# Outer spectrum stored row by row, the inner transform and the mixing in 128-channel pieces, and a new order of steps

## The reference, cut to what matters

```
# layer 0, per image: 7x7 depthwise convolution, LayerNorm over channels, two linear maps with GELU, residual
h = conv7x7(x) + b;  h = LN(h);  x = (gelu(h @ w1 + b1) @ w2 + b2) * layer_scale + x
# layer 1, on tokens t (3136 x 96)
z = relu(bn1(LN(t) @ w1))                       # 3136 x 192
X = fft(z, axis=tokens, norm='ortho')
xr = relu(X.real * rd - X.imag * id + rb)       # rd, id: one number per channel (192)
xi = relu(X.imag * rd + X.real * id + ib)
y = ifft(xr + 1j * xi).real
t = t + bn2(y @ w2)                             # 192 -> 96 channels
t = t + qlinear(relu(qlinear(LN(t), W1)), W2)   # 96 -> 384 -> 96 with fp8 roundings
```

## Time and profile before

| what | value |
|---|---|
| median of 3 runs | 4494.48 us (4490.79 to 4496.14) |
| profiled execution, its own time | 4496.04 us |
| its span in the profile | 4494.2 us |
| PE, DVE, ACT, POOL busy | 4006.1, 3307.4, 2254.2, 1840.4 us |
| mean granted TensorE clock | 0.948 |

### The profile page before, as it was taken

The page is one execution under the profiler, slowest core; times in us unless marked ns, Lnnn a source line. Parts: engine busy times, 40 slices in busy tenths (PEclk is TensorE's granted clock), DMA queues, the critical chain, the costliest instruction groups (busy, mean ns, idle before and its releaser), DMA issues.

```text
span 4494.2 us, 88363 instructions
## 1 busy us (share of the span) xinstructions
PE 4006.1 (89%) x22802; PEld 2904.3 (65%) x22802; DVE 3307.4 (74%) x10713; ACT 2254.2 (50%) x4610; POOL 1840.4 (41%) x2468
## 2 busy tenths in 40 slices
PE   5999958899999999999999999999999999999986
PEld 3444435676666766676667676666666667676764
DVE  2333335688888888888888888888888888888877
ACT  2433423455555555555555555555555555555543
POOL 1111163444444444444444444444444444444431
PEclk9999979999999999999999999999999999999986
DMA  6566633444444444434444444444444444444331
GB/s 174 161 164 176 168 93 89 109 118 118 117 119 117 120 118 116 111 103 111 111 115 112 109 111 111 116 118 120 118 115 119 115 120 120 117 115 115 109 98 53
DMA packets 420415, 532.47 MB, mean 118 GB/s; under 512 B 220047, under 2 KB 378493, under 8 KB 404413
## 3 DMA queue, kind: packets, MB, share of 16 engines
q1 hardware_dynamic: 405920, 510.40, 42.4%
q10 hardware_dynamic: 14272, 20.04, 1.8%
HBM read 295.18 MB, written 235.12 MB: 118 GB/s over the span
## 4 chain that ended last, share of the span: by engine, by line
PE 29%; DVE 26%; DMA 13%; issue 10%; ACT 3%; SPq 2%; POOL 1%; DVEq 1%; ACTq 0%; POOLq 0%
DMA inner<-outer_spectrum 6%; PE psum L989 6%; DMA outer_spectrum<-outer 6%; DVE stats L823 5%; PE psum L1009 5%; PE psum L1028 4%; PE psum L995 4%; DVE minus L898 4%; DVE plus L898 3%; DVE t L859 3%; PE psum L1037 2%; DVE h L932 2%; DVE xn L925 2%; PE psum L1017 2%; DVE act L881 2%
## 5 line engine op out<-in xcount | busy, mean ns | idle before, releaser
L684 POOL TENSOR_TENSOR scales<-sums,minus_half 112x4 f32<-112x4 f32 (+1 forms) x480 | 605.8, 1266 | 1686.2 <-DVE sums L839 1685.7
L726 POOL TENSOR_TENSOR both<-plus,minus 96x224 f32<-96x224 f32 (+1 forms) x1024 | 642.7, 653 | 356.6 <-DVE minus L898 297.8
L781 ACT ACTIVATE uw<-psum,spec 96x224 f32<-96x224 f32 (+1 forms) x1024 | 449.4, 512 | 397.9 <-PE psum L1028 395.9
L989 PE MATMUL psum<-hn,w_sb 96*128 96x448 f32 x1344 | 566.3, 559 | 31.8 <-ACT hn L747 31.8
L995 PE MATMUL psum<-hid,w_sb 128*96 128x448 f32 x1344 | 554.7, 549 | 2.1 <-ACT hid L762 2.0
L762 ACT ACTIVATE hid<-psum,b_sb 128x448 f32<-128x448 f32 x672 | 421.3, 634 | 233.3 <-PE psum L989 192.0
L387 PE MATMUL c_psum<-c_xt,c_toeplitz 128*112 128x448 f32 x1152 | 477.9, 552 | 49.2 <-ACT c_xt L329 26.0
L1028 PE MATMUL psum<-inner_dft,inner 112*96 112x112 f32 x3712 | 431.2, 271 | 90.5 <-DMA inner<-outer_spectrum 89.8
L415 DVE TENSOR_SCALAR c_h<-c_psum,c_bias 112x448 f32<-112x448 f32 x192 | 199.0, 1037 | 415.1 <-PE c_psum L387 415.1
L701 POOL TENSOR_SCALAR h_norm<-h,sums,scales 112x96 f32<-112x96 f32 x896 | 461.3, 531 | 103.2 <-PE psum L982 102.9
L1028 PEld LDWEIGHTS psum<-inner_dft,inner 112*96 112x96 f32 x3712 | 406.0, 173 | 110.9 <-issue 86.4
(11 more groups left out here) (85 smaller groups left out, 6615.0 us busy)
## 6 DMA issues: line engine op xcount, KB each, us to landing
outer_spectrum<-outer SPq DMA_DIRECT2D x448, 168.0 KB
inner<-outer_spectrum SPq DMA_DIRECT2D x32, 2016.0 KB
c_xpad<-x SPq DMA_DIRECT2D x96, 392.0 KB, 11.2
h_tokens<-c_h SPq DMA_DIRECT2D x24, 1568.0 KB, 8.4
h<-h_tokens SPq DMA_DIRECT2D x32, 1176.0 KB, 13.9
x_sb<-x SPq DMA_DIRECT2D x32, 1176.0 KB, 7.7
residual_stream<-t SPq DMA_DIRECT2D x224, 168.0 KB, 2.0
inner_inverse<-unmixed SPq DMA_DIRECT2D x224, 168.0 KB, 2.3
```

Source lines behind the costliest of these rows:

```text
L684: nc.gpsimd.tensor_tensor(scales[which][:, at:at + w], su[:, :, 5], minus_half[:, 0:w], ALU.pow).then_inc(ready.sem, 1)
L726: last = nc.gpsimd.tensor_tensor(both[:, c % 2, m, 0:w, k * PT // 2:(k + 1) * PT // 2], half(plus), half(minus), ALU.subtract if k else AL ...
L781: last = nc.scalar.activation(uw[:, j % 2, k, 0:w * PT // 2].rearrange("p (s k) -> p s k", s=w), re, ACT.Identity, bias=spec[:, m, shift:s ...
L989: pe.matmul(bank("M1", c, m, CW, 128), w1_sb[:, m * 128:(m + 1) * 128], hn[:, c * CW:(c + 1) * CW], start=True, stop=True).then_inc(m1_mad ...
```

## The change

Six things are changed together.

1. `outer_spectrum` in DRAM becomes (28 q, 116 rows, 192) in place of (114 rows, 28 q, 192). The rows of the outer transform are laid out so that 29 rows that belong to one partition of `inner` follow each other. A store of a chunk of A is two transfers in place of three (pieces of 768 B in place of 3072 B). The load of `inner` is two transfers in place of three: 8 rows (6144 B for each of 112 partitions), then 21 rows (16128 B each), in place of 4 rows, 24 rows and one row in pieces of 768 B.
2. B works on two rows at a time, whose 2 x 192 channels are cut in three blocks of 128: channels 0 to 127 of the first row, the last 64 of the first with the first 64 of the second, the last 128 of the second (three "kinds"). There are 12 steps of up to four blocks of one kind: 44 matmuls for a turn in place of 58, and 12 steps on ACT, DVE and POOL in place of 16, on 128 partitions in place of 96.
3. W sums the kinds: for two rows a matmul of 96 columns from kind 0, one of 96 columns from kind 2 and one of 192 columns from kind 1 (its weights have zeros in half of the rows for each output). 44 matmuls in place of 58: 30 of 96 columns and 14 of 192.
4. The outer transform has 116 columns in place of 114.
5. The table of the outer transform is loaded in the convolution's first microseconds, between the loads of the first and the second part of x, and put in the new order by four DVE copies; the small weight loads are some more (55 in place of 42).
6. `STAGES` and `LATER` have new numbers throughout.

```diff
-    g_dram = nc.dram_tensor("outer_spectrum", (2 * K1, NQ, H2), F32, kind="Internal").ap()
+    g_dram = nc.dram_tensor("outer_spectrum", (NQ, ROWS, H2), F32, kind="Internal").ap()
...
-    2: {"B": (8.0, 8.7, ND), "W": (18.0, 9.9, ND), "IB": (27.5, 8.9, ND)},
+    2: {"B": (0.5, 4.7, KINDS * NG), "W": (18.0, 9.9, ND), "IB": (32.5, 8.7, ND)},
...
-    "sp": {"M2": -2.0, "IB": -0.5, "A": 12.0, "FETCH": -8.0, "FETCH NEXT": 10.5},
+    "sp": {"M2": 20.5, "IB": 2.5, "A": 7.0, "FETCH": -6.5, "FETCH NEXT": 12.5},
...
-                        for rows, part in ((slice(0, PT, 2), slice(0, K1 - 1)), (slice(1, PT, 2), slice(K1, 2 * K1 - 1)),
-                                           (slice(PT, 2 * K1), slice(K1 - 1, 2 * K1, K1))):
-                            sp.dma_start(g_dram[rows, CH * c:CH * c + CH, :], outer[part, c % 2, :, :]
+                        for rows in (slice(0, PT), slice(PT, ROWS)):
+                            sp.dma_start(g_dram[CH * c:CH * c + CH, rows, :].rearrange("q m h -> m q h"), outer[rows, c % 2, :, :]
                                          ).then_inc(outer_stored[c % 2].sem, 16)
...
-                        for part, (first, end) in enumerate(((0, CH), (CH, NS - 1))):
-                            rows = bass.AP(g_dram.tensor, first * PT * H2, [[H2, PT], [PT * H2, end - first], [1, H2]])
-                            sp.dma_start(inner[:, first:end, :], rows).then_inc(inner_loaded[part].sem, 16)
-                        sp.dma_start(inner[0:2 * NQ, NS - 1, :], g_dram[2 * K1 - 2:2 * K1, :, :].rearrange("m q h -> (m q) h")
-                                     ).then_inc(inner_loaded[1].sem, 16)
+                        spectrum = g_dram.rearrange("q (r s) h -> (q r) (s h)", s=NS)
+                        first = 2 * PAIRS * H2
+                        for part, columns in enumerate((slice(0, first), slice(first, NS * H2))):
+                            sp.dma_start(inner[:, columns], spectrum[:, columns]).then_inc(inner_loaded[part].sem, 16)
...
-                        w = chunk_pairs(c)
-                        for m in range(2):
-                            dst = bank("B", c, m, w * PT, C, "spec")
-                            for s in range(w):
-                                last = pe.matmul(dst[:, s * PT:(s + 1) * PT], inner[:, CH * c + s, m * C:(m + 1) * C],
-                                                 inner_dft[:, :], start=True, stop=True)
-                            last.then_inc(spec_made.sem, 1)
+                        w = blocks(g, kind)
+                        dst = bank("B", c, 0, w * PT, 128, "spec")
+                        for u in range(w):
+                            at = 128 * (KINDS * (PAIRS * g + u) + kind)
+                            last = pe.matmul(dst[:, u * PT:(u + 1) * PT], inner[:, at:at + 128], inner_dft[:, :],
+                                             start=True, stop=True)
+                        last.then_inc(spec_made.sem, 1)
...
+                        for u in range(chunk_pairs(c) // 2):
+                            two = dst[:, u * H2:(u + 1) * H2]
+                            pe.matmul(two[:, 0:C], both[:, g % 2, 0, first + u, :], aw2_sb[:, 0:C], start=(u == 0), stop=False)
+                            pe.matmul(two[:, C:H2], both[:, g % 2, 2, first + u, :], aw2_sb[:, C + H2:], start=False, stop=False)
+                            last = pe.matmul(two, both[:, g % 2, 1, first + u, :], aw2_sb[:, C:C + H2], start=False,
+                                             stop=(u == PAIRS // 2 - 1))
```

More of the change, by code:

```diff
@@ L25 @@
 ND = (NS + CH - 1) // CH
+NG = (ND + 1) // 2
+PAIRS = 4
+KINDS = 3
+ROWS = 4 * NS
 CC = 4
@@ L46, in chunk_pairs, with blocks @@
     return min(CH, NS - CH * d)
+def blocks(g, kind):
+    pairs = min(PAIRS, NS // 2 - PAIRS * g)
+    return pairs + (NS % 2 if g == NG - 1 and kind < 2 else 0)
 class Signal:
@@ L407, in _ @@
             dve.wait_ge(consts_loaded, 32)
+            dve.wait_ge(transform_loaded, 16)
+            columns = transform.rearrange("p (q m) -> p q m", m=2 * K1)
+            for j in range(2):
+                for part_ in range(2):
+                    at, count = NS * (2 * j + part_), NS - j
+                    nc.vector.tensor_copy(wts.outer_dft[0:PT, :, at:at + count],
+                                          columns[:, :, K1 * part_ + j:K1 * (part_ + 1):2])
+                    if j:
+                        nc.vector.memset(wts.outer_dft[0:PT, :, at + count:at + NS], 0.0)
             def part(n, g, slot, has_next, has_second):
@@ L489, in image_phase @@
         t1_fetched = [signal(f"t1_fetched{k}", len(range(k, NC, 3)), 16, first=2) for k in range(3)]
-        outer_stored = [signal(f"outer_stored{n}", 4 - n, 48) for n in range(2)]
-        inner_loaded = [signal(f"inner_loaded{part}", 1 + part, 16) for part in range(2)]
+        outer_stored = [signal(f"outer_stored{n}", 4 - n, 32) for n in range(2)]
+        inner_loaded = [signal(f"inner_loaded{part}", 1, 16) for part in range(2)]
         unmixed_stored = [signal(f"unmixed_stored{n}", ND // 2, 16, first=1) for n in range(2)]
@@ L1031, in turn @@
-                    if name == "W":
-                        w = chunk_pairs(c)
-                        dst = bank("W", c, 0, w * C, PT)
-                        pe.wait_ge(both_done.sem, both_done.at(n, 2 * c + 1))
-                        for s in range(w):
-                            for m in range(2):
-                                last = pe.matmul(dst[:, s * C:(s + 1) * C], both[:, c % 2, m, s, :],
-                                                 aw2_sb[:, m, :], start=(m == 0), stop=(m == 1))
+                        g, kind = c // KINDS, c % KINDS
@@ L1225, in fold_batch_norms @@
     count = 1
-    for bn, sc, half in ((raw.bn1, raw.scale1, raw.halves[:, :]), (raw.bn2, raw.scale2, raw.halves[0:C, 0:C])):
+    for bn, sc, half in ((raw.bn1, raw.scale1, raw.halves[0:PT, :]), (raw.bn2, raw.scale2, raw.halves[:, 0:C])):
         steps = [
```

181 lines of the change are left out of this document (97 added, 84 removed), and 6 rows, old and new, of the table LATER.

## The result

The changed kernel takes 4603.35 us, median of 4 runs (4600.73 to 4624.78), the kernel before 4495.31 in the same comparison (4490.79 to 4496.47). The ratio is 1.025, 95% interval 1.0225 to 1.0274: 2.5% slower. The forecast was 4542, with 4400 to 4605 as its range. The direction came out, and so did the mechanism at the turn's start; of the span's growth, 106.3 us (4600.5 for 4494.2), the forecast had 48.

A forecast was written before the change was run, and what follows sets the result against it. PE's work was taken to bound the long part, the order of transfers the turn's start. 4496 + 54 for 30 turns - 7 for other turns + 1 for the convolution's start gave 4544, as runs' median 4542; range 4400 to 4605.

The forecast's parts named there:

- What bounds the kernel: A turn has a long part, where PE's list sets the time, and a start, where the order of transfers counts.
- The line: Turn's start: x_sb, `back`, A6's store, `inner` and t_old land in series; S20 starts 31.2 us after A5's matmuls end.
- I take 11.0: Turn's start: the load of `inner` takes 11.0 us, with 9.5 as the range's lower value, where before it took 12.3.
- The long part: From S20 to the end of A5's matmuls: 87.3 us, with PE barely ahead of DVE.
- The turn: Turn's start 31.2 plus long part 87.3 gives 118.5 us for 116.7; 30 turns give +54.
- The ends: Turns without the long line save about 7 us in all; the convolution's start costs +1.
- A: Rival, turn's start: shorter transfers bring S20 at 27.5 us after A5's matmuls; 113.8 us a turn, 4403; chance 0.38.
- B: Rival, whole turn: both effects cancel, S20 at 29.6 us after A5's matmuls; 116.9 us a turn, 4496; chance 0.09.
- C: Rival, long part: DVE sets it at 90 us and PE's clock falls; 121.5 us a turn, 4634; chance 0.07.
- D: Rival, turn's start: large pieces don't make `inner` faster than 12.3 us; 4583; chance 0.46 together with the forecast.
- The signs named: Whole turn: DVE idle some 20 us before AP0, serial transfers, B's records 0.096 us, x_sb issues 118 us apart, PE below 89%.

The follow-up runs named there:

- e1: Changed kernel with the three t_old fetches for the next turn ahead of A6's store on SP: 4566.4 us.
- e4: Kernel before with its t_old fetches for the next turn put behind `inner` on SP: 4784.3 us.
- e7: Changed kernel with x_sb's load ahead of IB5's and A4's stores on SP, and the t_old fetches ahead of A6's store: 4397.9 us.
- e8: As e7, with the t_old fetches also ahead of IB7's store and `back` on SP: 4336.1 us, the changed kernel's best order.
- f7: e8 with A6's step earlier on SP, so its store and `inner` went ahead of IB7's store and `back`: 4803.8 us.
- e12: Kernel before with 128 stationary columns for 96 in 56 of B's 58 matmuls: 10 us less than the kernel before.
- f4: Kernel before with 18 of B's 58 matmuls done twice on PE: 40 us more.
- f5: Changed kernel with the 15 matmuls of B's first kind done twice on PE: 31 us more.
- f2: Changed kernel's layout, kinds and matmuls in the order table of the kernel before, only B's entry new: 4473.7 us.
- f1: Changed kernel with `inner` loaded in pieces of 768 B, by five transfers for two: 4672.3 us.
- run 97: Not a run's label: the 97 us are the PE time that f5 put into the changed kernel, for 31 us more.
- f6: Changed kernel with DVE writing 112 more columns, not read, in each block of B: 73 us more.

## Why the prediction was partly right

**What bounds the kernel.** Right for the turn's start, which was read as one line of transfers. e1 to e4, e7, e8 and f7 all move the time by moving members of it. Not borne out for the long part: by "there PE's list sets the time", work put on PE there had to cost its full time, and e12, f4 and f5 got nothing to half of it.

**The line.** x_sb at T + 2.1 (2.2 measured), `back` 11.0 (10.7), `inner` 18.7 (19.3), AP0's sum 30.5 (32.1). Two terms were too small. `inner` with t_old behind it: "I take 11.0" and 0.8 were 11.8, and 12.7 were measured. And 8.6 instead of 7.7 went by between the issues of `back` and `inner`; the terms named for this step, 4.6 + 1 + 1.4, make only 7.0. The first part of `inner` lands 5.4 us after its issue, the second at 11.7, which is 12.1 after the first issue:

```profile
inner<-outer_spectrum SPq DMA_DIRECT2D x32, 1764.0 KB, 11.7
...
t_old<-residual_stream SPq DMA_DIRECT2D x224, 168.0 KB, 8.6
...
inner<-outer_spectrum SPq DMA_DIRECT2D x32, 672.0 KB, 5.4
```

The rate of the data was right, 264 GB/s or 9.4 us; what lies around them is 2.7 us, and 1.6 were allowed. The rows held a warning: from the issue of `inner` to AP1's sum, whose t_old stands behind it, and the earlier trace rows show 2141.65 - 2127.66 = 14.0 us, where the prediction says 12.5.

**The long part.** 87.3 from S20, 88.0 from AP0's sum, were predicted, 87.2 from that sum measured. This is in part luck. B's record was taken at 0.096 and is 0.112 in the changed kernel, so its 88 records cost 9.9 us for 8.4, more than the 9.3 of the upper bound; and the sum counts PE's work alone. W takes 1.44 us in the timeline (2157.94 to 2159.38 in e8) for 1.56, seven times and a last one of 0.5, so 10.6 (predicted 10.5).

**The turn.** 118.5 predicted, 119.6 measured. From the second T of the run to the last, 30 turns took 85 us more than before, for the 54 of the forecast: 31 us of the 58 that it lacks.

**The ends.** This is the step that failed outright: "about 7 in all" saved in the turns without the long line, and 1 us for the convolution's start, so -6. Measured by T, the ends cost 21 us, the other 27. The first T comes 12.5 us later (741.5 for 729.0), 9.5 of which are there at the first issue of x_sb (649.4 for 639.9). The turn after it, the one without part 3, is 5.7 us shorter (94.6 for 100.3), as the prediction has it. But from the last T to the end of the span it is 14.2 us longer (178.3 for 164.0). That stretch is 165.3 in f2, which has the new work in the old table, and still 174.9 in e8, whose line is short: the end pays for the new order table, and mostly not by way of the line. The prediction priced these turns by the work alone and put the order at nothing in them. Which entry of the table it is stays open.

**The rivals.** A (the line is short) didn't come, but its ground was half right, since the large pieces are faster (f1). The earlier trace rows hinted at it: `back`, in pieces of 10.5 KB, moved its 264 GB/s with the DMA engines 0.88 busy, `inner`, in pieces of 768 B, its 251 at 1.06. B didn't come. C's premise, DVE as the limit, is borne out as little as PE's, and its price (90 us for the long part) was too high; nor was the clock of 0.94, from which it priced the stops, a typical one (0.88). D (large pieces make nothing faster) gave 4583, nearest to 4603, and f1 refutes its reason; its 12.3 comes near the 12.1 that `inner` took by luck, for counted from the first issue the load of before took about 13.3.

**The signs named.** DVE idle some 20 us before AP0, ended by t_old: 20.8 in the turn shown, 658.8 us in 31 times. Transfers one behind the other: yes. PE's share below 89%: 86. Distance of 118 us between issues of x_sb: 119.6. B at 0.096: no.

## What to carry to other kernels

When a queue carries both large loads and small transfers that something waits for, read the order of its issues before the busy shares: a change that saves work on every engine lost 2.5% with the large load of x_sb just ahead of a store that SP waits for and the small fetches behind `inner`, and was 3.6% faster than before once both had been moved up. Look also at what stands ahead of the waiting instruction on the other engines, and at which wait would take the place of the one that you remove: a late t_old was worth 37 us in one kernel and 291 in the other. And to learn what an engine's time is worth, put some in and look in which stretch it lands: over the whole run 97 us more of PE gave 31 and 92 us more of DVE 73, but within the long part both cost about 0.8 of themselves.

## What the runs showed of the hardware

- A small transfer lands the later, the more bytes were issued ahead of it: 42 KB took 2.3 us in e7, 3.5 in e8, 7.9 in the changed kernel behind x_sb, 11.9 in f7 behind `inner`.
- With the DMA engines full, the load of `inner` ran at 264 GB/s in pieces of 6 and 16 KB and at 235 in pieces of 768 B (changed kernel and f1, means over the turns).
- A record of B with 112 moving columns takes 0.096 us with 96 stationary columns and 0.112 with 128 (kernel before and e12), and e12, with 27 us more in PE's busy total, was no slower.
- With the longer stops of PE at the turn's start the granted clock fell: 0.84 in that stretch for 0.88 (medians of the turns); over the run the mean went from 0.948 to 0.924, and to 0.951 in e8, whose stops are short.
- PE's busy time grew by 0.9 us a turn in the long part of f6, in which only DVE had more to do.
